# Causal mask of the first group by TensorE, and a reordered end of the last layers, in a float32 decoder

## Chip, cores, metric

One core of one Trainium2 chip. The time is the device time of one execution of the whole decoder in microseconds; lower is better. Everything is float32.

## What is computed

A decoder of two blocks on x (8 x 256 x 256): attention, cross attention and a mixture of experts, then the second block, with which the change is concerned. Each of its layers is followed by the sum with its input and a layer norm:

```
# second block: gated attention (16 heads of 16), MLP inside it, cross attention, channel mix
scores = einsum('bqhd,bkhd->bhqk', q, k) / sqrt(16)
scores = where(tril, scores, -inf);  attn = softmax(scores);  out = attn @ v
...
x_prev = concat([0, x[:, :-1]], axis=1)
xr = mu_r * x + (1 - mu_r) * x_prev
xk = mu_k * x + (1 - mu_k) * x_prev
out = sigmoid(xr @ W_r.T) * (square(relu(xk @ W_k.T)) @ W_v.T)
x = layernorm(x + out)
```

## The kernel before

The second block is one function, `last_layers`. The 2048 rows are 4 groups (G = 4) of 2 batch items, so a group has 4 tiles of 128 rows (NT = 4, HALF = 2). The groups go through a software pipeline of three stages: in period p group p is in attention (a), group p-1 in output product and MLP (r), group p-2 in cross attention and channel mix (z). Each engine has its own written program, a function per engine (`sync`, `gpsimd`, `tensor`, `scalar`, `vector`), strictly in order; semaphores join them (`wait_ge`, `then_inc`). The names of engines below are PE (TensorE), DVE (VectorE), ACT (ScalarE), POOL (GpSimd), SP.

*First group's attention (period 0).* Nothing else is in the pipeline yet, and the group is worked off in two halves, one batch item each. A half has 8 score units of 2 heads (`scores`, L1830 on). Unit j has the pair of banks 2(j mod 2) and the next one; its 4 products contract 32 rows each, so heads in different strips of 32 rows of the array can run side by side. Each bank gets 384 score columns (CAUSAL): 256 queries against the first 128 keys, 128 queries against the others. The two diagonal blocks of 128 x 128 are masked by DVE (`minimum`, L2889 on: the minimum with a tile of 3e38 and -1e30, in place in PSUM, 4 blocks a unit). Then ACT takes the exponential of the unit (`exponential`, L2442 on) and frees the banks (`s1e`). After every second unit but two steps late PE forms the weighted sum of values (`weighted`, L1846 on, bank 4), and ACT copies it (`heads_copy`). Before a half the PE turns the rotated queries and keys (`first_turns`, L1991) and DVE multiplies them with the gates' factors (`factors`, L2816 on). DVE's program of the first half holds the 8 minimums between its preparation of the second half (square sums, rotation, clock, norms); in the second half each minimum is followed by one `combine` (L2767) of the next group's rows, gathered from the experts' output by POOL. Then follow statistics, norm and turn of that front (`front_statistics`, `front_normalise`, ACT's `front_rows` L2398, PE's `turn_front`).

```
for j in range(PAIRS1 // GB, PAIRS1):      # DVE, second half of group 0
    minimum(0, j)
    combine(1, j - PAIRS1 // GB)
```

ACT's factors for the second half (`first_factors(1)`, L2515 to L2521) stand behind its eighth exponential. The flag `const` of POOL says that the masks and the ones in the values' tile are ready.

*The end.* After the periods the last group (LAST = 3) and the one before (OTHER = 2) are worked off with a program of their own. For the channel mix of the last group: PE turns the normed rows into a bank, ACT copies them shifted by one column (`mix_rows`, L2688), POOL subtracts shifted from unshifted (`last_difference`, L1758), DVE forms both mixes from the difference (`last_mix`, L3188), PE multiplies (`last_keys`, `last_receptance`), ACT takes relu and tanh (`last_activations`), DVE squares (`last_squares`, L3195), PE multiplies with W_v (`last_values`), and DVE forms the result (`last_result`, L3202 to L3207), statistics, and after POOL's root (`rstd`, L1667 and L1669) the norm (`last_norm`, L3181). Each step does one batch item, that is 2 tiles. The norm of OTHER stands in DVE's program between the results.

## Time and profile before

| | |
|---|---|
| median of 3 runs | 1203.19 us (1202.64 to 1204.02) |
| profiled execution, its own time | 1208.58 us |
| its span, first to last instruction | 1206.8 us |
| PE, DVE, ACT, POOL busy | 1103.5, 722.0, 548.7, 457.3 us |
| mean granted clock of PE | 0.967 |

### The profile page before, as it was taken

What the parts mean: (1) busy time and instruction counts of PE and PEld (TensorE: products, weight loads), DVE (VectorE), ACT (ScalarE), POOL (GpSimd) and SP (SyncE); (2) the same over time, 40 slices, a digit from 0 to 9 for tenths busy, and PEclk for the clock granted to TensorE, in tenths of its full rate; (3) what the DMA queues carried; (4) which work ended last, traced back from release to release, by engine and by line L of the source; (5) the groups of instructions that cost most, each with busy time, mean ns of one, the idle gap of its engine ahead of it and who ended that gap; (6) DMA issues with size and microseconds to landing.
All of it is one profiled execution on the core that took longest, in us unless ns stands there. A gap on an engine that the chain in (4) does not pass through costs nothing. (4 is left out here: it accounts for less than half of the span.)

```text
span 1206.8 us, 20429 instructions
## 1 busy us (share of the span) xinstructions
PE 1103.5 (91%) x6772; PEld 795.2 (66%) x6772; DVE 722.0 (60%) x2206; ACT 548.7 (45%) x1391; POOL 457.3 (38%) x535
## 2 busy tenths in 40 slices
PE   9899989998998997999999977789799899998996
PEld 4476457546744776999999964455565665565874
DVE  1482476348434845656565638658858787946456
ACT  1371265217322824333333337466576557643541
POOL 0160034006300974766666456025332432223022
PEclk9999999999999998999999989689999999999999
DMA  6000200020002033941111154000000100000001
GB/s 207 18 2 1 59 19 1 0 60 19 1 0 60 2 115 119 310 141 53 45 54 45 41 165 126 2 1 23 14 1 17 36 9 19 8 1 19 1 1 35
DMA packets 39997, 55.85 MB, mean 46 GB/s; under 512 B 6758, under 2 KB 32166, under 8 KB 39894
## 3 DMA queue, kind: packets, MB, share of 16 engines
q1 hardware_dynamic: 30598, 39.61, 10.1%
q0 software_dynamic: 3408, 9.31, 2.8%
q10 hardware_dynamic: 5888, 5.64, 1.5%
q8 instruction: 55, 0.90, 0.3%
q14 instruction: 48, 0.39, 0.1%
HBM read 43.76 MB, written 10.78 MB: 45 GB/s over the span
## 5 line engine op out<-in xcount | busy, mean ns | idle before, releaser
L1787 PE MATMUL bank<-words 128*128 128x256 f32 (+3 forms) x872 | 270.1, 461 | 20.4 <-ACT words L2391 3.7
L1787 PEld LDWEIGHTS bank<-words 128*128 128x128 f32 (+1 forms) x872 | 164.8, 196 | 99.2 <-issue 58.9
L464 PE MATMUL bank<-words 128*128 128x512 f32 x384 | 171.6, 595 | 0.1
L409 POOL TENSOR_TENSOR words<-words 128x256 f32<-128x256 f32 (+1 forms) x128 | 102.5, 829 | 151.8 <-DVE words L1090 151.2
L1297 PEld LDWEIGHTS bank<-words 128*128 128x128 f32 x1248 | 145.9, 193 | 3.5 <-ACT words L1333 1.6
L1297 PE MATMUL bank<-words 128*128 128x128 f32 x1248 | 146.4, 276 | 0.9 <-ACT words L1333 0.9
L787 ACT ACTIVATE words<-words 128x128 f32<-128x128 f32 (+1 forms) x256 | 112.8, 443 | 32.1 <-DVE words L923 32.0
L464 PEld LDWEIGHTS bank<-words 128*128 128x128 f32 x384 | 71.2, 191 | 78.6 <-issue 78.3
L779 ACT ACTIVATE words<-bank 128x512 f32<-128x512 f32 x48 | 28.7, 597 | 178.1 <-PE bank L464 178.1
L1348 ACT ACTIVATE words<-words 128x1024 f32 x39 | 41.1, 1057 | 137.1 <-PE bank L1297 98.4
L913 DVE COPY words<-bank 128x512 f32<-128x512 f32 x48 | 33.2, 691 | 92.2 <-PE bank L464 91.9
L923 DVE CUSTOM_DVE_ANT_0 words<-bank,words 128x128 f32<-128x128 f32 (+1 forms) x256 | 74.5, 349 | 7.2 <-PE bank L475 7.1
L1308 PE MATMUL bank<-words 128*128 x312 | 73.9, 380 | 0.7 <-DVE words L1397 0.7
L934 DVE COPY words<-bank 128x512 f32<-128x512 f32 x96 | 60.8, 685 | 15.8 <-PE bank L488 15.4
L475 PE MATMUL bank<-words 64*128 64x128 f32 (+1 forms) x512 | 54.2, 347 | 11.3 <-DVE words L923 7.9
L1254 POOL COPY words<-words 128x1024 f32 x39 | 40.3, 1035 | 60.3 <-PE bank L1297 60.3
L2447 ACT ACTIVATE words<-bank 128x768 f32<-128x768 f32 x64 | 48.9, 811 | 28.6 <-DVE bank L2892 28.4
L1308 PEld LDWEIGHTS bank<-words 128*128 128x128 f32 x312 | 56.2, 190 | 7.1 <-issue 1.1
L2892 DVE TENSOR_TENSOR bank<-bank,words 128x512 f32<-128x512 f32 x64 | 42.0, 693 | 27.9 <-PE bank L1842 25.9
L1393 DVE TENSOR_SCALAR words<-bank,words 128x128 f32<-128x128 f32 x156 | 44.0, 345 | 24.1 <-PE bank L1297 23.8
L130 POOL TENSOR_TENSOR words<-words 128x4 f32<-128x4 f32 x6 | 1.2, 202 | 148.2 <-DVE words L112 148.2
L488 PE MATMUL bank<-words 128*128 128x128 f32 x384 | 51.8, 282 | 6.1 <-POOL words L409 5.8
(357 smaller groups left out, 2003.5 us busy)
## 6 DMA issues: line engine op xcount, KB each, us to landing
words<-in_w SPq DMA_DIRECT2D x8, 1024.0 KB
y_slots<-words ACTq DMA_DIRECT2D x39, 128.0 KB
words<-in_w SPq DMA_DIRECT2D x8, 512.0 KB
words<-in_x SPq DMA_DIRECT2D x4, 512.0 KB, 4.1
x_rows<-words SPq DMA_DIRECT2D x16, 128.0 KB, 1.8
words<-in_wm SPq DMA_DIRECT2D x2, 1024.0 KB, 7.6
out_x<-words SPq DMA_DIRECT2D x16, 128.0 KB, 1.8
words<-in_xt SPq DMA_DIRECT2D x3, 512.0 KB, 3.8
```

Source lines behind the costliest of these rows:

```text
L409: last = pool.tensor_tensor(part, part, inv[:, j % SLOTS0, :, t:t + 1].to_broadcast([P, 2, P * (t + 1)]), ALU.mult)
L464: last = pe.matmul(bank[c % 2][:, :], w, r, start=k == 0, stop=k == KD - 1)
L475: last = pe.matmul(bank[SCORES[i % 2][n]][:, t * P:t * P + P * (t + 1)],  kt[r, m, b * S + t * P:b * S + (t + 1) * P], qt[r, m, b * S:b * ...
L488: last = pe.transpose(bank[2 + k][:, tok(i)], weights_of(j)[:, n, c:c + P], ident[:, :])
L787: last = act.activation(weights_of(i)[:, n, c], weights_of(i)[:, n, c], ACT.Exp, bias=negmax[:, i % SLOTS0, n, t:t + 1], scale=-1.0, accum ...
L923: last = dve.tensor_tensor_reduce(out=weights_of(i)[:, n, c], in0=bank[SCORES[i % 2][n]][:, c], in1=mask0[:, c], scale=-DH0 ** -0.5, scala ...
L934: dve.tensor_copy(turning[:, 512 * k:512 * k + 512], bank[2 + k][:, :]).then_inc(tcopied, 1)
L1297: last = pe.matmul(bank[(BANKG, BANKV)[half][j % 2]][:, c * P:(c + 1) * P], wfix[:, j % 2, k * 2 * FF + half * FF + c * P:k * 2 * FF + hal ...
L1308: last = pe.matmul(bank[BANKY[j % 2]][:, 0:D], hidden[:, j % 2, k * P:(k + 1) * P], w2[:, bass.ds(e * W2 + k * D, D)], start=k == 0, stop= ...
L1393: dve.tensor_scalar(value[:, c * P:(c + 1) * P], bank[BANKV[s]][:, c * P:(c + 1) * P], bias[:, bass.ds(e * 2 * FC + FC + c, 1)], 10.0, ALU ...
L1787: last = pe.matmul(out, w, r, start=i == 0, stop=i == len(pairs) - 1)
L2447: act.activation(es[:, j % 4, :, :], pair(j % 2)[:, :, 0:CAUSAL], ACT.Exp, scale=DH1 ** -0.5).then_inc(s1e, 1)
```

## The change

*Masks.* A new tile `below` (384 columns: 0 where a key may be seen, -1e30 where not, in both diagonal blocks) is filled by POOL with the other constants; it lies in the tile of the MLP, which is free until period 1. For group 0 `minimum` is gone. Instead PE starts each of a unit's two banks with a product of the identity and `below`, and the scores are summed onto it; the scores increment `s1m`, for which ACT waits. DVE's combines of group 1 now stand in a row. Groups 1 to 3 keep `minimum`.

*The end.* The mix of the last group is formed as mu x + (1 - mu) x_prev: ACT writes mu x from the turned bank (4 operations per batch item, behind its shifted copy), DVE adds (1 - mu) x_prev; POOL's difference is gone. ACT does both copies and activations batch by batch. DVE's order is a new one, with the statistics of OTHER moved up between the adds, and a mix between two adds. The norm of OTHER is applied by POOL. PE's receptance of batch 0 goes ahead of the turn of batch 1. The second batch item's values, result, statistics, root and norm go by tile.

```diff
@@ constants, POOL
+                pool.memset(below[:, :], 0.0)
...
+                for c in (slice(0, P), slice(S, CAUSAL)):
+                    pool.affine_select(out=below[:, c], in_=below[:, c], compare_op=ALU.is_ge,
+                                       fill=-1e30, base=0, pattern=[[1, P]], channel_multiplier=-1)
@@ end, POOL
-            def last_difference(b):
-                pool.wait_ge(n7.copied, 2 * LAST + b + 1)
-                pool.tensor_tensor(lastrl[:, :, batch(b)], x5t[:, :, b, 1:S + 1], x5t[:, :, b, 0:S], ALU.subtract).then_inc(lastapart, 1)
+            def older_norm(b):
+                rstd(OTHER, n8, b)
+                pool.drain()
+                for t in range(HALF * b, HALF * b + HALF):
+                    pool.tensor_scalar(x(OTHER, t), x(OTHER, t), n8.mv[:, t, 0:1], n8.inv[:, t:t + 1], ALU.subtract, ALU.mult).then_inc(n8.normed, 1)
...
+            rstd(LAST, n7, 0)
+            older_norm(0)
+            rstd(LAST, n7, 1)
+            older_norm(1)
+            rstd(0, n9, 0)
+            for t in rows_of_last:
+                last_rstd(t)
@@ PE
-                        last = pe.matmul(bank[n][:, part], ktm[r, odd, k0:k0 + P], qt[r, m, queries], start=True, stop=True)
-                last.then_inc(s1, len(units))
+                        last = pe.matmul(bank[n][:, part], ktm[r, odd, k0:k0 + P], qt[r, m, queries],
+                                         start=not masked, stop=keys == P or not masked)
+                last.then_inc(s1m if masked else s1, len(units))
...
+            def masked_scores(j):
+                if j >= 2:
+                    pe.wait_ge(s1e, j - 1)
+                for o in range(2):
+                    pe.matmul(bank[2 * (j % 2) + o][:, 0:CAUSAL], ident[:, :], below[:, :], start=True, stop=False)
+                scores(0, (j,), True)
...
-                        scores(0, (PAIRS1 // GB * b + j,))
+                        masked_scores(PAIRS1 // GB * b + j)
...
             last_keys(0, 6)
+            last_receptance(0, 7)
             last_turn(n7, 1, bank[5])
-            last_receptance(0, 7)
             last_values(0, 4)
             last_keys(1, 0)
             last_receptance(1, 2)
-            last_values(1, 5)
+            pe.wait_ge(lastkact, 2)
+            for t in rows_of_last:
+                product(bank[LASTVALUE[t]][:, 0:D], [(lastrl[:, k, tok(t)], wv2[:, k, :]) for k in range(KD)]).then_inc(lastv, 1)
@@ ACT
+            def scaled_rows_of(b, source):
+                for mu, dst in ((MUK, lastxk), (MUR, lastxr)):
+                    for k in range(KD):
+                        last = act.activation(dst[:, k, batch(b)].rearrange("p (t n) -> p t n", t=HALF), turned_rows(bank[source])[:, k, :, :],
+                                              ACT.Copy, scale=cols[:, mu, k:k + 1])
+                    last.then_inc(lastscaled, 1)
@@ DVE, first group
-            minimum(0, 0)
-            minimum(0, 1)
             square_sums(0, 2)
...
             for j in range(PAIRS1 // GB, PAIRS1):
-                minimum(0, j)
                 combine(1, j - PAIRS1 // GB)
@@ DVE, end
+            def last_mix(b, mu, dst):
+                dve.wait_ge(lastscaled, 2 * b + (1 if mu == MUK else 2))
+                for k in range(KD):
+                    last = dve.scalar_tensor_tensor(dst[:, k, batch(b)], x5t[:, k, b, 0:S], rest[:, mu - MUR, k:k + 1],
+                                                    dst[:, k, batch(b)], ALU.mult, ALU.add)
+                last.then_inc(lastmixed, 1)
...
+            statistics(OTHER, n8, rows_of_tiles(0))
             normalise(LAST, n7, lambda t: x(LAST, t), 0)
             add_product(LAST, n7, 2, bank[0])
+            last_mix(0, MUK, lastxk)
             add_product(LAST, n7, 3, bank[2])
-            last_mix(0)
+            last_mix(0, MUR, lastxr)
             normalise(LAST, n7, lambda t: x(LAST, t), 1)
+            last_squares(0, 6)
             older_result(1)
+            statistics(OTHER, n8, rows_of_tiles(1))
+            last_mix(1, MUK, lastxk)
+            last_mix(1, MUR, lastxr)
+            first_result(4)
             last_squares(1, 0)
+            last_statistics(rows_of_tiles(0))
+            for t in rows_of_last:
+                last_result(t)
+            for t in range(NT):
+                dve.wait_ge(n9.rstd, max(t, 1))
+                dve.tensor_scalar(x(LAST, t), x(LAST, t), n9.mv[:, t, 0:1], n9.inv[:, t:t + 1], ALU.subtract, ALU.mult).then_inc(n9.normed, 1)
```

Where the instructions stand. First PE's program at the start of the second half of the first group's attention, before; L1991 is the turn, L1842 the scores, L1853 the weighted sum, `x2` a repetition:

```order
L1991 MATMUL bank<-words 128x128 x8
L1842 MATMUL bank<-words 128x256 x2
L1842 MATMUL bank<-words 128x128 x2
L1842 MATMUL bank<-words 128x256 x2
L1842 MATMUL bank<-words 128x128 x2
L1842 MATMUL bank<-words 128x256 x2
L1842 MATMUL bank<-words 128x128 x2
L1842 MATMUL bank<-words 128x256 x2
L1842 MATMUL bank<-words 128x128 x2
L1853 MATMUL bank<-words 32x256 x4
L1853 MATMUL bank<-words 32x128 x4
```

and in the changed kernel, whose L2010, L1860 and L1872 are the same operations and L2018 the masks:

```order
L2010 MATMUL bank<-words 128x128 x8
L2018 MATMUL bank<-words 128x384 x2
L1860 MATMUL bank<-words 128x256 x2
L1860 MATMUL bank<-words 128x128 x2
L2018 MATMUL bank<-words 128x384 x2
L1860 MATMUL bank<-words 128x256 x2
L1860 MATMUL bank<-words 128x128 x2
L2018 MATMUL bank<-words 128x384 x2
L1860 MATMUL bank<-words 128x256 x2
L1860 MATMUL bank<-words 128x128 x2
L2018 MATMUL bank<-words 128x384 x2
L1860 MATMUL bank<-words 128x256 x2
```

Two mask products of 384 columns now stand ahead of the scores of each unit, and no two units stand side by side any more.

DVE in the second half, before: L2825 factors, L2892 minimum, L2767 combine:

```order
L2825 SCALAR_TENSOR_TENSOR words<-bank,words 128x2x128 x2
L2892 TENSOR_TENSOR bank<-bank,words 128x4x128
L2767 SCALAR_TENSOR_TENSOR words<-words 128x256
L2892 TENSOR_TENSOR bank<-bank,words 128x4x128
L2767 SCALAR_TENSOR_TENSOR words<-words 128x256
L2892 TENSOR_TENSOR bank<-bank,words 128x4x128
L2767 SCALAR_TENSOR_TENSOR words<-words 128x256
```

and now, L2861 factors, L2803 combine, L2942 and L2950 the statistics of the front:

```order
L2861 SCALAR_TENSOR_TENSOR words<-bank,words 128x2x128 x2
L2803 SCALAR_TENSOR_TENSOR words<-words 128x256 x8
L2942 BN_STATS words<-words 128x6 x2
L2950 BN_AGGR words<-words 128x2 x2
L2952 TENSOR_SCALAR words<-words 128x2
```

The combines stand in a row with nothing from PE to wait for.

The end of DVE's program, from the last adds of the cross attention (L2787, L2789) on, before; L3188 is the mix, L3234 and L3236 the result of OTHER, L3195 the squares, L3202 and L3204 the result, L3207 its statistics:

```order
L2797 BN_AGGR words<-words 128x2 x2
L3188 SCALAR_TENSOR_TENSOR words<-words 128x256 x4
L2781 TENSOR_SCALAR words<-words 128x256 x2
L3234 SCALAR_TENSOR_TENSOR words<-words,bank 128x512
L3236 SCALAR_TENSOR_TENSOR words<-words 128x512
L3188 SCALAR_TENSOR_TENSOR words<-words 128x256 x4
L3195 TENSOR_TENSOR words<-bank,words 128x2x256
L2774 BN_STATS words<-words 128x6 x2
L2797 BN_AGGR words<-words 128x2 x2
L2774 BN_STATS words<-words 128x6 x2
```

and the same part now; L3208 is the mix, L2817 the norm, L3215 the squares, L3268 and L3270 the result of OTHER, L2810 the statistics of OTHER:

```order
L3208 SCALAR_TENSOR_TENSOR words<-words 128x256 x2
L2823 TENSOR_TENSOR words<-bank,words 128x256
L2825 BN_STATS words<-words 128x6
L2833 BN_AGGR words<-words 128x2 x2
L3208 SCALAR_TENSOR_TENSOR words<-words 128x256 x2
L2817 TENSOR_SCALAR words<-words 128x256 x2
L3215 TENSOR_TENSOR words<-bank,words 128x2x256
L3268 SCALAR_TENSOR_TENSOR words<-words,bank 128x512
L3270 SCALAR_TENSOR_TENSOR words<-words 128x512
L2810 BN_STATS words<-words 128x6 x2
L2833 BN_AGGR words<-words 128x2 x2
L3208 SCALAR_TENSOR_TENSOR words<-words 128x256 x4
```

The keys' mix of batch 0 stands between two adds, and its squares ahead of the result of OTHER.

## Rows read from the trace of the kernel before

**Rows 1.** Page, costliest groups: line engine op count | busy us, mean ns, idle us.

```profile
L1787 PE MATMUL bank<-words 128*128 128x256 f32 (+3 forms) x872 | 270.1, 461 | 20.4 <-ACT words L2391 3.7
L1787 PEld LDWEIGHTS bank<-words 128*128 128x128 f32 (+1 forms) x872 | 164.8, 196 | 99.2 <-issue 58.9
```

**Rows 2.** Timeline, first score units: start us, length us, engine, line, form [idle before].

```profile
748.37 0.95 PE L1842 MATMUL bank<-words 32*128 32x256 f32 x16 [2.12 <-issue]
749.34 1.30 DVE L2892 TENSOR_TENSOR bank<-bank,words 128x512 f32<-128x512 f32 x2 [1.02 <-PE bank L1842]
```

**Rows 3.** Stretches: us, busy of PE, PEld, DVE, ACT, POOL; granted clock, DMA.

```profile
750.90:757.80 6.90, 6.86 (x64) 4.69 (x64) 5.12 (x10) 3.21 (x5) 1.27 (x1) 0.51 0.01 2
761.20:781.70 20.50, 14.48 (x126) 9.41 (x124) 13.36 (x26) 8.20 (x15) 0.00 (x0) 0.50 0.00 1
785.10:795.30 10.20, 6.18 (x34) 4.23 (x35) 6.12 (x25) 4.68 (x11) 2.25 (x3) 0.50 0.00 0
847.30:870.20 22.90, 19.32 (x242) 13.15 (x242) 19.06 (x44) 10.90 (x18) 8.87 (x11) 1.00 0.02 7
```

**Rows 4.** Chain of waits near the end: start us, us, what (256-column passes).

```profile
1134.53 10.56 PE bank L1787 x48
```

**Rows 5.** Timeline of PE, second period: 8 passes of 512 columns at full clock.

```profile
878.09 3.60 PE L1787 MATMUL bank<-words 128*128 128x512 f32 x8
```

**Rows 6.** Timeline of PE: two units and a sum (847 us), one unit (760 us).

```profile
847.31 0.93 PE L1842 MATMUL bank<-words 32*128 32x256 f32 x16 [0.83 <-issue]
848.17 0.86 PE L1853 MATMUL bank<-words 128*32 128x256 f32 x16
...
760.40 0.94 PE L1842 MATMUL bank<-words 32*128 32x256 f32 x8 [1.53 <-ACT words L2447]
761.27 1.51 PE L1853 MATMUL bank<-words 128*32 128x256 f32 x16
```

**Rows 7.** Timeline, between the halves of the first group's attention.

```profile
763.05 1.51 ACT L2447 ACTIVATE words<-bank 128x768 f32<-128x768 f32 x2 [2.43 <-DVE bank L2892]
...
767.06 1.94 PE L1991 MATMUL bank<-words 128*128 128x128 f32 x8 [0.57 <-DVE words L3007]
770.64 1.68 PE L1842 MATMUL bank<-words 32*128 32x256 f32 x16 [1.63 <-DVE words L2825]
```

**Rows 8.** Timeline, from the last weighted sum to the front's turn.

```profile
785.90 1.51 PE L1853 MATMUL bank<-words 128*32 128x256 f32 x16 [1.76 <-ACT words L2440]
...
787.47 0.38 ACT L2440 ACTIVATE words<-bank 128x256 f32<-128x256 f32 x1 [1.71 <-PE bank L1853]
...
789.87 0.91 ACT L2398 ACTIVATE words<-words 128x256 f32<-128x256 f32 x2 [2.02 <-DVE words L2933]
...
791.75 1.12 PE L1796 MATMUL bank<-words 128*128 128x128 f32 x4 [0.20 <-ACT words L2398]
```

**Rows 9.** Timeline, the end of the kernel.

```profile
1184.98 1.64 DVE L3188 SCALAR_TENSOR_TENSOR words<-words 128x256 f32<-128x256 f32 x4
...
1185.97 1.97 PE L1787 MATMUL bank<-words 128*128 128x256 f32 x8 [2.22 <-DVE words L3188]
...
1189.09 1.04 POOL L1758 TENSOR_TENSOR words<-words 128x512 f32<-128x512 f32 x1 [2.71 <-ACT words L2688]
...
1192.49 7.40 PE L1787 MATMUL bank<-words 128*128 128x256 f32 x32 [2.39 <-DVE words L3195]
...
1203.82 0.74 DVE L3181 TENSOR_SCALAR words<-words 128x256 f32<-128x256 f32 x2 [0.60 <-POOL words L1669]
```

**Rows 10.** Timeline, ACT's scaled copies of 128x256 from PSUM.

```profile
715.68 1.02 ACT L2359 ACTIVATE words<-bank,words 128x256 f32<-128x256 f32 x2 [0.53 <-PE bank L1796]
```

**Rows 11.** Timeline, POOL's selects and ACT's first copy behind the flag.

```profile
720.29 0.29 POOL L1652 TENSOR_SCALAR_AFFINE_SELECT words<-words 128x128 f32<-128x128 f32 x1
...
728.79 0.39 ACT L2429 ACTIVATE words<-bank 128x256 f32<-128x256 f32 x1
```

**Rows 12.** POOL by shape before 700 us, columns as in rows 1.

```profile
L392 POOL TENSOR_SCALAR words<-words 128x128 f32<-128x128 f32 x24 | 19.1, 794 | 0.0
```

More of the change, by code:

```diff
@@ L1436, in last_layers @@
         ones, tiny = sb([P, S]), sb([P, 1])
+        rest = sb([P, 2, KD])
         mask1, maskx = sb([P, P]), sb([P, S2])
@@ L1494, in last_layers @@
         m1pair, m1gelu, lastxq, lastxqr, lastbias = (sem("l_" + n) for n in ("m1pair", "m1gelu", "lastxq", "lastxqr", "lastbias"))
-        lastapart, lastmixed, lastkmm, lastrelu, lastkact, lastrmm, lastrsig, lastv, lastvr = (sem("l_last" + n) for n in (
-            "apart", "mixed", "kmm", "relu", "kact", "rmm", "rsig", "v", "vr"))
+        lastscaled, lastmixed, lastkmm, lastrelu, lastkact, lastrmm, lastrsig, lastv, lastvr = (sem("l_last" + n) for n in (
+            "scaled", "mixed", "kmm", "relu", "kact", "rmm", "rsig", "v", "vr"))
         PAIRS1, QUADS1 = GB * H1 // 2, GB * H1 // 4
@@ L1504, in last_layers @@
         LASTUP, LASTDOWN = ((4, 5, 0, 2), (1, 3, 4, 5)), (0, 2, 1, 3)
+        LASTVALUE = (4, 4, 5, 6)
         NE1, NW, NR = 5, 10, 5
@@ L1530, in rows_of @@
             return slice(HALF * b, HALF * b + HALF)
+        rows_of_last = range(HALF, NT)
         def batch(b):
@@ L1774, in _ @@
             last_bias(1)
-            for b in range(2):
-                rstd(LAST, n7, b)
-                last_difference(b)
-            for b in range(2):
-                rstd(OTHER, n8, b)
-            for b in range(2):
-                rstd(0, n9, b)
+            rstd(LAST, n7, 0)
[5 more added lines that the diff above has]
+                last_rstd(t)
         @block.tensor
@@ L1828, in form, with scores @@
                 product(bank[4 + i % 2][:, :], [(w[:, k, tok(c % 2)], xnt[:, k, :]) for k in range(KD)]).then_inc(fmm, 1)
-            def scores(g, units):
+            def scores(g, units, masked=False):
                 q = units[0] // 2
@@ L2751, in _ @@
             sums_copy(LAST, 3, (0, 2))
-            mix_rows(LAST, 0, 4)
-            mix_rows(LAST, 1, 5)
-            last_activations(0, 6, 7)
-            last_activations(1, 0, 2)
+            for b in range(2):
+                mix_rows(LAST, b, 4 + b)
+                scaled_rows_of(b, 4 + b)
+                last_activations(b, (6, 0)[b], (7, 2)[b])
         @block.vector
@@ L3175, in rows_of_tiles @@
                 return range(HALF * b, HALF * b + HALF)
-            def last_norm(b):
-                dve.wait_ge(n9.rstd, b + 1)
-                for t in rows_of_tiles(b):
-                    dve.tensor_scalar(x(LAST, t), x(LAST, t), n9.mv[:, t, 0:1], n9.inv[:, t:t + 1], ALU.subtract, ALU.mult).then_inc(n9.normed, 1)
-            def last_mix(b):
-                dve.wait_ge(lastapart, b + 1)
-                for mu, dst in ((MUK, lastxk), (MUR, lastxr)):
-                    for k in range(KD):
-                        last = dve.scalar_tensor_tensor(dst[:, k, batch(b)], lastrl[:, k, batch(b)], cols[:, mu, k:k + 1],
-                                                        x5t[:, k, b, 0:S], ALU.mult, ALU.add)
-                    last.then_inc(lastmixed, 1)
+            def last_mix(b, mu, dst):
[4 more added lines that the diff above has]
+                last.then_inc(lastmixed, 1)
             def last_squares(b, source):
@@ L3195, in last_squares, with first_result, last_statistics, last_result @@
                 dve.tensor_tensor(lastrl[:, :, batch(b)], both(source, b), lastrl[:, :, batch(b)], ALU.mult).then_inc(lastkact, 1)
-            def last_result(b, source):
-                h = slice(NT * LAST + HALF * b, NT * LAST + HALF * b + HALF)
-                dve.wait_ge(lastrsig, b + 1)
-                dve.wait_ge(lastv, b + 1)
-                dve.scalar_tensor_tensor(lastrs[:, rows_of(b), :], lastrs[:, rows_of(b), :], 1.0, both(source, b), ALU.add, ALU.mult)
+            def first_result(source):
+                h = slice(NT * LAST, NT * LAST + HALF)
+                dve.wait_ge(lastrsig, 1)
+                dve.wait_ge(lastv, 1)
+                dve.scalar_tensor_tensor(lastrs[:, 0:HALF, :], lastrs[:, 0:HALF, :], 1.0, both(source, 0), ALU.add, ALU.mult)
                 dve.drain()
-                dve.scalar_tensor_tensor(keep["x"][:, h, :], lastrs[:, rows_of(b), :], 0.5, keep["x"][:, h, :], ALU.mult, ALU.add)
+                dve.scalar_tensor_tensor(keep["x"][:, h, :], lastrs[:, 0:HALF, :], 0.5, keep["x"][:, h, :], ALU.mult, ALU.add)
                 dve.drain()
-                for t in rows_of_tiles(b):
+            def last_statistics(tiles):
+                for t in tiles:
                     dve.bn_stats(n9.bn[:, t, :], x(LAST, t))
-                averages(n9, rows_of_tiles(b))
+                averages(n9, tiles)
+            def last_result(t):
+                dve.wait_ge(lastrsig, 2)
+                dve.wait_ge(lastv, t)
+                dve.scalar_tensor_tensor(lastrs[:, t, :], lastrs[:, t, :], 1.0, bank[LASTVALUE[t]][:, 0:D], ALU.add, ALU.mult)
+                dve.drain()
+                dve.scalar_tensor_tensor(x(LAST, t), lastrs[:, t, :], 0.5, x(LAST, t), ALU.mult, ALU.add)
+                dve.drain()
+                last_statistics((t,))
+            dve.tensor_scalar(rest[:, :, :], cols[:, MUR:MUK + 1, :], -1.0, 1.0, ALU.mult, ALU.add)
             for t in range(NT):
```

25 lines of the change are left out of this document (7 added, 18 removed).

## Prediction

> **What bounds the kernel now.** The page first: the costliest group is PE's products, 872 passes with an idle time before them that is small, 20.4 us [rows 1], so work added to PE costs its own length unless PE waits at that place. Then the order of instructions in time, in the two places that the diff touches.
>
> *First group's attention (748 to 787 us).* A score unit is one pair of banks. Its cycle is PE, VectorE (DVE), ScalarE (ACT), PE: the scores are ready, DVE takes the minimum with the mask (two units in 1.30 us [rows 2]), ACT exponentiates (two in 1.51 us [rows 7]), and only then the pair of banks is free. PE waits here, and its granted clock stands at 0.50 to 0.51, the lower of its two levels (1.2 of 2.4 GHz), in most of both halves; in the later groups, whose attention is filled with the MLP's products, it is 1.00 [rows 3]. So this stretch is a ring of short dependent steps at half clock, not one of PE at its peak.
>
> *The end (1184 to 1207 us).* The shift by one token goes ACT, POOL, DVE, PE: after the last copy POOL subtracts for 1.04 us, then DVE mixes, PE had waited 2.39 us for the squares behind that mix, and after the last product, whose passes end at 1192.49 + 7.40 = 1199.89, DVE works to 1203.82 + 0.74 = 1204.56, a two-tile chain with POOL's root in it [rows 9].
>
> **Masks on PE, first half of the group.** Removed: 8 minimums of 0.65 us (1.30/2) from DVE [rows 2]. Added: 2 products of the identity with a 384-column mask per unit. A 256-column pass at full clock takes 10.56/48 = 0.22 us [rows 4] and a product is two passes; a 512-column pass 3.60/8 = 0.45 us with the last one's tail in it [rows 5]. 384 columns lie between: 0.22 x 1.5 = 0.33, 0.45 x 0.75 = 0.34, and as some of both is tail I take 0.325 us, so 4 passes or **1.3 us a unit**, 16 units 21 us of PE. At half clock it would be twice.
>
> The Trainium skill (TensorE: Matmul & The Clock Gate, section The mechanism) says that a weight load overlaps a running matmul only where the row groups differ; by that, each of the 64 passes would pay its load too. The trace disagrees: the 48 passes of [rows 4] use all rows, and 0.22 us each is no more than their columns take at 2.4 GHz.
>
> Scores: two units together take 848.17 - 847.31 = 0.86 us, but one unit alone also takes 761.27 - 760.40 = 0.87 us [rows 6], since its two row groups run side by side and the other two are idle. A full-array mask between the units ends that pairing. So a unit is 1.3 + 0.87 = 2.17 us. A weighted sum is 0.86 us long, about 0.8 us to the next start (my reading of the same rows; at half clock it is 1.51).
>
> The exponential of unit j and PE's work on unit j+1 overlap, and 2.17 us is longer than the 0.81 us of ACT, so PE never waits for a bank: it is the bound. The eighth unit's scores start 8 x 1.3 + 7 x 0.87 + 2 x 0.8 = 18.1 us after 748.37, its exponential starts 0.97 us later (the unit's 0.94 [rows 6] and a hand-over of 0.03, like the one of 748.37 + 0.95 to 749.34 [rows 2]), takes half of 1.51 and some, 0.81, and ends at 768.25; now that is 763.05 + 1.51 = 764.56 [rows 7]. **+3.7 us.** ACT's factors for the second half stand behind the eighth exponential, so what DVE is freed of (8 x 0.65 = 5.2 us) buys nothing here: DVE will wait for ACT.
>
> **Between the halves.** From that exponential to the next scores there are 770.64 - 764.56 = 6.1 us, with two turns of 1.94 us at half clock [rows 7]. PE comes to them warm, after two weighted sums: **-0.5 us** (none to -1).
>
> **Second half.** PE alone: 8 x 2.17 + 3 x 0.8 + 0.1 + 0.86 = 20.7 us. Now it is 785.90 + 1.51 - 770.64 = 16.8 us [rows 7, 8]. **+3.9 us.** But before it PE is nearly idle for some 4 us as DVE makes the factors, and after such idling the clock has been at its lower level here [rows 3]. I take 4 us at the lower level, which do 2 us of work: **+2.0 us** (0 to 3.4).
>
> **After the last weighted sum.** Now DVE's minimums and combines of the second group's rows alternate, statistics come last, and the turn of the front ends at 791.75 + 1.12 = 792.87, 5.4 us after the last sum's end [rows 8]. With the minimums gone, DVE has the whole second half for combines of the second group's rows, statistics and norm, all under PE's 20.7 us. What is late next is ACT, whose four row copies stand behind its last heads copy: 0.05 + 0.38 + 4 x 0.455 (two take 0.91, [rows 8]) + 0.5 = 2.8 us. **-2.6 us.** What follows PE did at 0.50 until 795.3 [rows 3]; warm, some of it shrinks: **-0.6 us** (0 to -1.2).
>
> **Constants.** POOL gets one fill and two more selects, 0.29 us each [rows 11], ahead of the flag; ACT's first copy that waits for it comes at 728.79, some 8 us after [rows 11]. Nothing, unless POOL is late by that much.
>
> **The end.** Each hand-over and DVE step here is read from the same part of the timeline as [rows 9]. Batch 0: ACT's two new copies with a scale take 1.02/2 = 0.5 us each from PSUM [rows 10], so after the shifted copy (which ends near 1182.7, 0.6 us after the turn) the keys' half is ready near 1183.7, and DVE mixes it in 0.82 us (half of 1.64) already between two adds, from 1183.9 on; PE's keys start near 1184.8, not 1185.97 [rows 9]. They end at 1186.6; the receptance, 1186.9 to 1188.7, the turn of batch 1 and the values of batch 0 follow without a stop. The norm of tiles 2 and 3 slips 0.7 us in return, as an add and the receptance mix now stand before POOL's root. POOL gets the older group's norms, 2 per batch; 128 columns of such an operation take it 0.79 us [rows 12], 256 of them perhaps 0.8 to 1.6; before its next root it has 4 us. Batch 1: PE is done with batch 0 by 1190.9; ACT copies from 1189.4 (after the turn and its tanh of 0.6 us), scales until 1190.95 and 1191.95; DVE, which in the meantime does the older result and its statistics, mixes until 1193.05; PE's keys and receptance, 16 passes of 0.23 (7.40/32), end at 1195.8 where they ended at 1199.89 less 8 such passes, about 1198.0. The values now come by tile, 4 passes or 0.9 us each: 1196.8 and 1197.7. DVE's work by tile is two products of 256 columns (0.42 each, by the first row of [rows 9]: 1.64/4), one bn_stats and one aggregation, and the hand-overs; I estimate 1.7 us: 1198.55 and 1200.25; then POOL's root, 1.2 us with its hand-overs as now, under which the first three tiles are normalised, and the last tile at 1201.5 to 1201.9. Now 1203.82 + 0.74 = 1204.56 [rows 9]. The stores behind are as before. **-2.7 us** (-4.2 to +0.5).
>
> **Sum.** +3.7 - 0.5 + 3.9 + 2.0 - 2.6 - 0.6 - 2.7 = **+3.2 us**. The profiled execution, 1208.58 us, would be 1211.8; it lies 5.4 us above the median, 1203.19, so the median would be **1206.4 us**. What a measurement of this kernel can tell from no change is 0.2%, 2.4 us: 1200.8 to 1205.6.
>
> **Rivals.**
> - *Faster, by packing.* If the score passes and the sums follow the masks without the hand-over that [rows 6] show, a unit's scores cost only their columns, (0.44 + 0.22) = 0.66 us, and the sums the same: -(15 x 0.21 + 5 x 0.14) = -3.9 us; PE is then dense enough that the pause between the halves leaves the clock up: -2.0. Together 3.2 - 5.9 = -2.7 us: 1200.5. For it: passes of one shape run without gaps [rows 4]. Against: one unit alone took 0.87 us at clock 1.00. It decides from 0.16 us a unit downward, given the clock. Chance 0.21. The Trainium skill (same page, section Why this matters for your kernels) asks for a PE that is not left idle between bursts if it is to keep its clock; by that the denser halves would gain, and no run so far tells whether the pause between them is short enough.
> - *No change.* The clock costs nothing (0 instead of +2.0) and the end gives 3.2: +0.7 us, 1203.9. Chance 0.26.
> - *More slower, at the end.* POOL's norms take 1.6 us and more beside DVE's work, the root of tiles 2 and 3 waits, and the gain at the end falls to 0.5: 1208.6. The Trainium skill (SBUF - State Buffer, section SBUF: two separate sides) says that POOL and DVE lock a shared pair of ports for a whole instruction, which would make this likelier; POOL's subtraction at 1189.09, beside idle DVE, took 1.04 us for 512 columns, so less than 0.8 us for 256 is likely, but no row has DVE busy beside it. Chance 0.10.
> - *Loads not hidden.* If a weight load of the page's 196 ns [rows 1] is paid on all 64 passes: +12.5 us, 1218.9. Chance 0.03.
> - *The masks themselves stay at half clock* (+21 us). 0.02: dense full-array passes have always come back to 1.00 in this trace.
>
> **How the numbers follow.** The forecast has 0.38; its own range, 1204.5 to 1209.5, comes from the unit's 2.1 to 2.25 us and the clock's 0 to 3.4. The range 1200.0 to 1211.0 takes in the first three rivals and the ends of the clock's term. Faster by over 0.2%: 0.21. Within: no change plus the low edge of the forecast, 0.30. Slower: 0.49.
>
> **What would show it.** In the changed kernel: mask products near 0.32 us a pass with the granted clock at 1.00; eighth exponential at 19 to 20 us after the first mask; DVE idle for ACT there; 18 to 23 us for the second half; 2.5 to 3.2 us from the last weighted sum to the end of the front's turn; the last DVE instruction 2 to 4 us nearer to the last context product. Wrong would be: PE waiting for ACT inside the halves, or mask passes at 0.65 us throughout.

## The result, and where the time went

The changed kernel takes **1213.62 us** (median of 4 runs, 1211.78 to 1214.80), the kernel before 1203.61 us beside it (4 runs, 1202.64 to 1205.56). The ratio is 1.0083, 95% interval 1.0069 to 1.0097: 10 us slower. The prediction had 1206.4 us in a range of 1200.0 to 1211.0. Its direction was right, its size and its range were not.

The profiled execution took 1214.54 us (span 1212.8). The stretches below are read from the timelines at the same events in both kernels. The second execution of the kernel before was profiled later, as `before_again`.

| stretch, us | before | before again | after | predicted change | measured change |
|---|---|---|---|---|---|
| half 1: first mask or scores to end of eighth exponential | 16.19 | 16.19 | 21.22 | +3.7 | +5.0 |
| to the next mask or scores | 6.08 | 6.07 | 5.73 | -0.5 | -0.35 |
| half 2: to the end of the last weighted sum | 16.77 | 16.76 | 28.81 | +5.9 | +12.0 |
| to DVE's first division behind the turn | 6.34 | 6.34 | 2.99 | -3.2 | -3.35 |
| all of periods 1 to 3 (not edited) | 383.8 | 377.5 | 380.2 | 0 | -3.6, +2.7 |
| end: first sum of the last cross attention to DVE's last end | 27.03 | 27.89 | 23.89 | -2.7 | -3.1, -4.0 |

The edited stretches add up to 5.0 - 0.35 + 12.0 - 3.35 - 3.1 = +10.2 us, close to the 10.0 us between the medians; the prediction's sum of the same terms was +3.2. How far this agreement is luck shows below, with `again`. Of the missing 7.0 us, 6.1 lie in half 2 and 1.3 in half 1.

PE in the changed kernel, from the timeline of PE (start us, length us, engine, line, form; in brackets the idle time before and what ended it):

```profile
747.56 1.56 PE L2018 MATMUL bank<-words 128*128 128x384 f32 x4 [2.20 <-DVE words L2861]
749.05 0.92 PE L1860 MATMUL bank<-words 32*128 32x256 f32 x8
749.90 1.56 PE L2018 MATMUL bank<-words 128*128 128x384 f32 x4
...
769.32 0.86 PE L1872 MATMUL bank<-words 128*32 128x256 f32 x16 [0.60 <-ACT words L2469]
771.40 1.17 PE L2010 MATMUL bank<-words 128*128 128x128 f32 x8 [1.22 <-DVE words L3043]
774.51 2.93 PE L2018 MATMUL bank<-words 128*128 128x384 f32 x4 [1.95 <-DVE words L2861]
777.37 1.65 PE L1860 MATMUL bank<-words 32*128 32x256 f32 x8
778.95 2.93 PE L2018 MATMUL bank<-words 128*128 128x384 f32 x4
...
802.46 0.86 PE L1872 MATMUL bank<-words 128*32 128x256 f32 x16 [0.60 <-ACT words L2469]
804.21 1.63 PE L1814 MATMUL bank<-words 128*128 128x128 f32 x8 [0.89 <-ACT words L2427]
```

The same stretch by windows (us; busy of PE, PEld, DVE, ACT, POOL with counts; granted clock; DMA share, GB/s): half 1 and the pause, the first part of half 2, the rest.

```profile
747.50:773.90 26.40, 23.19 (x168) 13.44 (x168) 13.13 (x23) 9.67 (x16) 3.81 (x3) 1.00 0.02 6
773.90:787.60 13.70, 13.09 (x36) 7.05 (x36) 8.78 (x30) 1.90 (x3) 2.27 (x3) 0.50 0.01 2
787.60:803.40 15.80, 15.12 (x128) 8.52 (x124) 0.00 (x0) 6.05 (x10) 0.00 (x0) 1.00 0.01 2
```

Three things stand here. The ring of [rows 2, 7] is gone: no row of a unit has an idle time before it, PE is the bound. In half 1 the clock is 1.00 where [rows 3] have 0.51 and 0.50, and still a unit takes 749.90 - 747.56 = 2.34 us, of which the masks are 749.05 - 747.56 = 1.49. And after the pause, in which PE has one row of turns between idle times of 1.22 and 1.95 us, the clock is at its lower level for 13.7 us, from 0.6 us ahead of the first mask on: a unit takes 778.95 - 774.51 = 4.44 us.

DVE has nothing left to do in half 1, and waits for ACT's factors (timeline, all engines):

```profile
767.97 0.81 ACT L2476 ACTIVATE words<-bank 128x768 f32<-128x768 f32 x1 [1.53 <-PE bank L1860]
...
769.96 0.69 DVE L3035 TENSOR_TENSOR words<-words 128x512 f32<-128x512 f32 x1 [12.54 <-ACT words L2546]
```

The end, in the places of [rows 9] (timeline, all engines):

```profile
1188.27 1.99 PE L1805 MATMUL bank<-words 128*128 128x256 f32 x8
...
1191.11 2.44 POOL L1776 TENSOR_SCALAR words<-words 128x256 f32<-128x256 f32 x2 [0.21 <-issue]
1191.56 1.56 ACT L2724 ACTIVATE words<-bank,words 128x256 f32<-128x256 f32 x4
...
1193.81 3.84 PE L1805 MATMUL bank<-words 128*128 128x256 f32 x16 [1.04 <-DVE words L3208]
...
1194.92 0.34 POOL L1676 TENSOR_TENSOR words<-words 128x2 f32<-128x2 f32 x1 [1.37 <-DVE words L2833]
...
1205.64 0.42 DVE L3237 SCALAR_TENSOR_TENSOR words<-words,bank 128x256 f32<-128x256 f32 x1 [0.36 <-PE bank L1805]
...
1207.24 0.42 DVE L3237 SCALAR_TENSOR_TENSOR words<-words,bank 128x256 f32<-128x256 f32 x1
...
1208.83 1.57 DVE L3316 TENSOR_SCALAR words<-words 128x256 f32<-128x256 f32 x4
```

The keys of batch item 0 (1193.81) and its receptance run in one row of 16 passes, where before the keys had a row of their own and a wait of 2.22 us. POOL's norm takes 2.44/2 = 1.22 us a tile and is done at 1193.55, 1.4 us before its next root. DVE's steps by tile are 1207.24 - 1205.64 = 1.60 us apart, and the last norm of four tiles is one row.

### The profile page after: what moved, and what is told of

Its sections match the earlier page's. It is cut to its first block and busy times, and to the rows that moved or that the text cites. A ratio compares the mean times of both kernels' runs of the same rounds, so it can differ in the third digit from the quotient of the medians.

```text
span 1212.8 us, 20562 instructions
## 1 busy us (share of the span) xinstructions
PE 1122.4 (93%) x6836; PEld 801.9 (66%) x6836; DVE 713.5 (59%) x2189; ACT 552.5 (46%) x1399; POOL 462.6 (38%) x542
## 3 DMA queue, kind: packets, MB, share of 16 engines
q1 hardware_dynamic: 30598, 39.61, 10.2%
## 5 line engine op out<-in xcount | busy, mean ns | idle before, releaser
L1676 POOL TENSOR_TENSOR words<-words 128x2 f32<-128x2 f32 x31 | 7.0, 226 | 144.1 <-DVE words L2833 144.0
```

## Which half of the change costs, and what the clock does

**The two parts by themselves.** `masks_only` has all edits but those of the end, `end_only` those of the end alone. Of the edit against the changed kernel two places stand here for each; the rest of it is the change's own diff taken back.

```diff
@@ masks_only: the end as before
-            last_receptance(0, 7)
             last_turn(n7, 1, bank[5])
+            last_receptance(0, 7)
...
@@ end_only: the masks as before
-                        masked_scores(PAIRS1 // GB * b + j)
+                        scores(0, (PAIRS1 // GB * b + j,))
...
+                minimum(0, j)
                 combine(1, j - PAIRS1 // GB)
```

> Only the masks move to TensorE; the end is that of before. Theory A (the masks cost 13 us, the end gives 3): 1216 to 1218 us, 12 to 14 us above before. Theory B (the end costs something too and the masks only some 10): 1211 to 1214 us.

> Only the end is new; the first group's masks stay with VectorE. Theory A: 3 us below before, 1200 to 1201.5 us, as the last VectorE instruction comes 3.1 us nearer to the last context products in the changed kernel's trace. Theory B: no gain or a loss, 1203 to 1205 us.

Beside 1207.54 us of the kernel before, `masks_only` took 1213.65 us (ratio 1.0051, 1.0031 to 1.0071) and `end_only` 1204.02 us (0.9973, 0.9957 to 0.9989). So the masks are the loss and the end a gain. As a difference, +6.1 us is less than either theory had for the masks, and -3.5 us is what theory A had for the end. The stretches give the sizes better than the ratios: with the old end the last stretch took 27.03, 27.89 and, in `masks_only`, 28.05 us, with the new one 23.9 in all 14 traces that have it. `masks_only` has the same 21.23 us in half 1 and 28.82 in half 2 as the changed kernel, `end_only` the 16.19 and 15.86 of the old ring. The ratios of the two parts, +0.51% and -0.27%, add up to less than the +0.83% of both together. The profiled execution of `masks_only` is no typical one: it is the slowest of seven, 1219.27 us at a mean granted clock of 0.976; only one other is like it (1218.35 us, 0.978), and the other five took 1209.87 to 1213.82 us at 0.982 to 0.985. These may have had a shorter stay at the lower clock, such as `again` shows below, but no trace shows them. Besides, the median of the kernel before itself lay between 1202.61 and 1208.37 us in the five comparisons, which is more than this gap: medians of different comparisons are not set against each other for a few us here.

**The same kernel again.** `again` and `third` are the changed kernel unedited, `before_again` the kernel before, for their traces.

> The changed kernel itself, timed beside the others of this call. 6 to 10 us above before.

> The changed kernel, a third trace: second half of the first group between 24 and 29 us as in the two others, the end 23.9 us from the first add of the cross attention to VectorE's last instruction.

> The kernel before once more, for a second trace: how much the stretch between the first group's attention and the end, which no part of the change touches, differs between two executions of one program. Theory: 2 to 4 us, all of it by the granted clock's dips; the first group's ring within 1 us of the first trace.

`again` took 1212.03 us (1.0078, 1.0064 to 1.0092); the single executions of `third` and `before_again` took 1216.00 and 1204.62 us. Half 1 is 21.23 us in all three traces of the changed kernel; half 2 is 28.81, 24.00 and 28.81. The windows of half 2 tell why (columns as above), of `again`:

```profile
775.00:778.85 3.85, 3.48 (x10) 1.74 (x12) 3.55 (x9) 0.00 (x0) 0.00 (x0) 0.57 0.01 4
778.85:799.60 20.75, 19.93 (x154) 11.37 (x150) 4.99 (x21) 8.09 (x13) 2.27 (x3) 1.00 0.01 2
```

and of `third`:

```profile
775.90:789.30 13.40, 12.77 (x34) 6.74 (x36) 8.80 (x30) 1.90 (x3) 2.26 (x3) 0.50 0.01 2
789.30:805.00 15.70, 15.10 (x126) 8.78 (x126) 0.00 (x0) 6.03 (x9) 0.00 (x0) 0.99 0.01 2
```

The clock falls in the pause every time. The windows that lie wholly at the lower level are, of `again` and of `third`,

```profile
774.90:778.30 3.40, 2.93 (x6) 1.25 (x6) 3.17 (x9) 0.00 (x0) 0.00 (x0) 0.50 0.02 5
775.93:789.57 13.64, 13.04 (x36) 7.01 (x36) 8.77 (x30) 1.90 (x3) 2.26 (x3) 0.50 0.01 2
```

so the way back took 3.4 us once and 13.6 us twice (in `masks_only` too), of the same instructions. One thing goes with it: the clock fell 0.60 to 0.62 us ahead of the first mask in the three traces with the long stay, and 0.48 to 0.49 us ahead of it in `again` and in the two spare runs below, which have the short one. No run moved this distance by itself, so it is not shown to be the cause.

With the short stay the edited stretches of `again` add up to 5.0 - 0.35 + 7.2 - 3.35 - 3.1 = +5.4 us, and yet this execution lies 9.2 us above the median before. Some 3.8 us of that come from stretches that no edit touches, which differ by as much between two executions of one program. So the equality of +10.2 and +10.0 above is in part luck. How many of the untraced executions of the changed kernel had the long stay is not known: of its nine timed in the two comparisons, five had a mean granted clock of 0.978 to 0.979 (1212.71 to 1214.80 us, the first profile among them) and four had 0.981 (1211.44 to 1212.03 us, `again` among them).

**Is it the pause?** `filler` puts products of no use (the identity with `below` into bank 5, which is free then) ahead of and behind the turns of the second half, 7 in all.

```diff
+            def filler(n):
+                for _ in range(n):
+                    pe.matmul(bank[5][:, 0:CAUSAL], ident[:, :], below[:, :], start=True, stop=True)
...
+                filler(3 * b)
                 pe.wait_ge(turning, HALF * b + HALF)
                 first_turns(b)
+                filler(4 * b)
                 pe.wait_ge(qkt, HALF * b + HALF)
```

> The changed kernel with 3 spare mask products (to an unused bank) before the turns of the second half and 4 behind them, so that TensorE is not idle while VectorE makes the factors. If the pause is what lets the clock fall, the granted clock stays at 1.00 in the second half, whose eight units then take 2.34 us each like the first half's: about 6.5 us less than the changed kernel, less at most 1 us that the filler delays the turns or scores: 1207 to 1209 us. If the clock falls for another reason (the masks themselves), it stays at 0.50 from 774 to 787 us and the time is 1213 to 1215 us.

Windows of `filler`: half 1, the pause, half 2.

```profile
750.00:772.00 22.00, 21.40 (x152) 12.32 (x156) 9.38 (x14) 8.35 (x14) 3.35 (x3) 1.00 0.02 7
772.00:777.00 5.00, 5.00 (x35) 3.26 (x28) 3.65 (x8) 1.21 (x3) 0.00 (x0) 1.00 0.01 3
777.00:801.00 24.00, 22.92 (x164) 13.06 (x162) 8.80 (x30) 8.35 (x14) 2.26 (x3) 1.00 0.01 1
```

PE is busy in all 5.00 us of the pause, and the clock stays at 1.00. Half 2 takes 22.51 us, the pause 6.82 instead of 5.73. This splits the 28.81: 22.5 is what the half takes with the masks at full clock, 6.3 the clock. Against the changed kernel the stretches give -6.3 + 1.1 = -5.2 us for the long stay at the lower level and -1.5 + 1.1 = -0.4 for the short one. By time it is 1208.89 us, ratio 1.0013 (0.9998 to 1.0028). The changed kernel was not timed beside it; `masks_only` was, at 1213.65 us, and less the 3.5 us of the end that is 1210.1 by estimate, 1.2 us above `filler`. So that the pause lets the clock fall is shown; what filling it is worth in the median lies between the two values. The Trainium skill (TensorE: Matmul & The Clock Gate, section Why this matters for your kernels) says that bursts of products must not be separated by idle gaps if the clock is to stay up. This pair of runs agrees, though that section speaks of longer single gaps than the two here, 1.22 and 1.95 us with a row of turns of 1.17 us between them.

**Is it what the products multiply?** Perhaps products of an identity and of zeros count for less than others. In `spare_dense` and `spare_mask` half 2 has two products of the same shape into bank 5 in place of the masks, of the MLP's weights or of identity and mask; DVE masks that half again. Both also wait for the weights ahead of the turns.

```diff
                 for o in range(2):
-                    pe.matmul(bank[2 * (j % 2) + o][:, 0:CAUSAL], ident[:, :], below[:, :], start=True, stop=False)
+                    if first_part:
+                        pe.matmul(bank[2 * (j % 2) + o][:, 0:CAUSAL], ident[:, :], below[:, :], start=True, stop=False)
+                    else:
+                        pe.matmul(bank[5][:, 0:CAUSAL], wm1[:, 0, 0:P], wm1[:, 0, P:P + CAUSAL], start=True, stop=True)
...
             for j in range(PAIRS1 // GB, PAIRS1):
+                minimum(0, j)
                 combine(1, j - PAIRS1 // GB)
```

> Second half of the first group: VectorE takes the minimum again (with its combines between), while TensorE computes in each unit, in place of the two mask products, two products of the same shape with dense weights and dense data, to an unused bank (one more wait for the weights). If the long time at the lower clock comes from mask products being almost all zeros, the clock is back at 1.00 within some 6 us of the first of them; if it comes from their shape, float32 and order, it stays at 0.50 for 10 to 13 us as in the changed kernel.

> The same with the identity and the mask as operands of the spare products. By both theories 10 to 13 us at 0.50 in the second half; time 1 to 3 us above the changed kernel. Against spare_dense it tells what the data does.

They took 1213.57 us (1.0088, 1.0073 to 1.0103) and 1211.09 us (1.0063, 1.0046 to 1.0081). The window after the pause, of `spare_dense`:

```profile
775.00:778.80 3.80, 3.41 (x8) 1.68 (x10) 0.33 (x1) 0.00 (x0) 0.00 (x0) 0.56 0.02 4
```

and of `spare_mask`:

```profile
774.70:777.50 2.80, 2.51 (x4) 1.18 (x4) 0.24 (x1) 0.00 (x0) 0.00 (x0) 0.50 0.03 6
```

Both were back after some 3 us, both had 24.6 us in half 2, and neither showed the 10 to 13 us at the lower level that was expected. The contents make no difference that these traces show. But both have the short stay, which the changed kernel has too in `again`, timed beside them; whether contents matter where the stay is long is not shown. Both also had 7.35 us behind the last weighted sum, where the changed kernel has 2.99: with the minimums back among the combines, DVE is late again. That is the term of -3.2 of the prediction, undone by itself.

## What a mask product costs

**Two units behind four masks.** `paired` makes the masks of two units in one go and then their scores.

```diff
-                for o in range(2):
-                    pe.matmul(bank[2 * (j % 2) + o][:, 0:CAUSAL], ident[:, :], below[:, :], start=True, stop=False)
-                scores(0, (j,), True)
+                for n in range(4):
+                    pe.matmul(bank[n][:, 0:CAUSAL], ident[:, :], below[:, :], start=True, stop=False)
+                scores(0, (j, j + 1), True)
```

> Masks of two units together, then the scores of both together. If each change between full-array masks and 32-row scores costs a hand-over of some 0.2 us and one unit's scores cost as much as two, a pair of units takes 8 x 0.32 + 0.2 + 0.86 = 3.6 us at full clock in place of 4.68: 4 us less per half, 1204 to 1207 us in all, if the clock behaves as in the changed kernel. If the hand-over isn't what the mask's 0.37 us per pass holds, and scores don't pair, no gain: 1212 to 1215 us.

Timeline of PE of `paired`, the first pairs:

```profile
746.58 2.85 PE L2018 MATMUL bank<-words 128*128 128x384 f32 x8 [2.12 <-DVE words L2861]
749.36 0.94 PE L1860 MATMUL bank<-words 32*128 32x256 f32 x16
751.92 2.85 PE L2018 MATMUL bank<-words 128*128 128x384 f32 x8 [1.63 <-ACT words L2476]
```

Eight passes take 2.78 us to the next start, four took 1.49. The difference, 1.29/4 = 0.3225 us, is the pass, as predicted (0.325). What is left, 1.49 - 4 x 0.3225 = **0.20 us**, comes once each time scores follow masks, and the prediction did not have it. The scores of two units run side by side again, in 0.87 us. Yet a cycle of two units is 751.92 - 746.58 = 5.34 us against 2 x 2.34 = 4.68 plus a weighted sum of 0.79 where there is one: now all four banks must be free before the masks start, so PE waits for ACT. Time 1209.25 us, ratio 1.0011 (0.9997 to 1.0024); neither expectation holds. Half 1 is as long as with the changed kernel (21.3 us), half 2 takes 25.63 us. The lower clock lasted 10.2 us, of which 6.2 lie in half 2 and the rest in the pause.

**Masks in bfloat16.** `bf16` multiplies bfloat16 copies of the identity and of the mask; the scores stay in float32.

```diff
+                pool.tensor_copy(below16[:, :], below[:, :])
+                pool.tensor_copy(ident16[:, :], ident[:, :])
...
-                    pe.matmul(bank[2 * (j % 2) + o][:, 0:CAUSAL], ident[:, :], below[:, :], start=True, stop=False)
+                    pe.matmul(bank[2 * (j % 2) + o][:, 0:CAUSAL], ident16[:, :], below16[:, :], start=True, stop=False)
```

> The changed kernel with the identity and the mask in bfloat16 (both exact there, -1e30 rounded), so a mask product is one pass of 384 columns. If it costs a quarter of the float32 one, 0.16 us, a unit takes 2 x 0.16 + 0.2 + 0.86 = 1.4 us at full clock, and a half of the group 14 us where before it took 16.2 to 16.8: 12 to 15 us below the changed kernel, 3 to 6 us below before. If a product has a floor or the clock stays low in both halves (PE less busy), no more than 5 us below the changed kernel.

Timeline of PE of `bf16`, a unit of half 1 and one of half 2:

```profile
748.88 0.50 PE L2024 MATMUL bank<-words 128*128 128x384 bf16 x2
749.31 0.92 PE L1866 MATMUL bank<-words 32*128 32x256 f32 x8
750.17 0.50 PE L2024 MATMUL bank<-words 128*128 128x384 bf16 x2
...
769.83 0.82 PE L2024 MATMUL bank<-words 128*128 128x384 bf16 x2
770.58 1.65 PE L1866 MATMUL bank<-words 32*128 32x256 f32 x8
```

and its window of half 2:

```profile
767.60:794.30 26.70, 25.21 (x149) 14.41 (x149) 6.91 (x26) 11.83 (x21) 2.26 (x3) 0.50 0.01 2
```

A product is one pass of half the length: two masks take 0.43 us instead of 1.49, a unit 1.29 instead of 2.34. Half 1 takes **12.77 us**, less than the 16.19 of DVE's ring. But half 2 takes 24.22 us: it begins at 766.10, the clock fell 1.1 us later, behind a pause of 5.73 us, and stayed down for all of this window, though PE was busy in 25.2 of its 26.7 us. The kernel is level with the one before, 1203.32 us, ratio 1.0008 (0.9991 to 1.0025).

**Both remedies.** `bf16_filler` adds 1 + 3 products in float32 around the turns to `bf16`; `bf16_paired_filler` makes the masks by pairs too; `both_fillers` has 3 more ahead of half 1; `bpf_again` repeats `bf16_paired_filler`. `end_filler` has the end's edits and DVE's old masks, with such products in the pause and behind each weighted sum.

```diff
@@ bf16_filler, bf16_paired_filler (both_fillers: filler(3, ...) in the first line)
+                filler(b, below[:, :])
                 pe.wait_ge(turning, HALF * b + HALF)
                 first_turns(b)
+                filler(3 * b, below[:, :])
@@ end_filler
                         weighted(0, QUADS1 // GB * b + (j - 3) // 2)
+                        filler(1, wqk[:, 0, 0:CAUSAL])
```

> The bfloat16 masks with spare float32 full-array products in the pause between the halves (1 before the turns, 3 behind them). In the run with the bfloat16 masks alone the clock fell in that pause and stayed at 0.50 for all of the second half, 24.2 us against 14.2 at full clock. If the pause is the cause: clock 1.00 all through, second half 14.2 us, 9 to 10 us below the bfloat16 masks alone: 1192 to 1195 us. If the 32-row scores themselves let it fall, it falls within the second half: 1198 to 1203 us.

> The same with two units' masks and then two units' scores together. A pair is then 4 x 0.16 + 0.2 + 0.86 = 1.7 us of TensorE, but waits for both exponentials, about 3.4 us a pair with the weighted sum against 2 x 1.28 + 0.8 = 3.36: the same time within 1.5 us as bf16_filler if the clock holds; with more pauses it may fall, then up to 8 us more.

> The masks stay with VectorE, the end is new, and spare float32 full-array products fill TensorE: 1 and 3 in the pause between the halves, one behind each weighted sum in both halves. If the lower clock is what costs the ring of before its time, the scores and sums run in half the time: 2 to 4 us below end_only, 1198 to 1202 us. If VectorE and ScalarE set the ring (the first half's minimums stand behind other work), no gain beyond 1 us.

> bf16_paired_filler with 3 spare float32 full-array products also in the pause ahead of the first half, where in the trace of bf16_filler the clock fell to 0.50 from 751 to 771 us (first half 20.4 us) and in others it did not. If that fall is what spreads the times, the clock is 1.00 in both halves in the trace and the median is 1 to 3 us below bf16_paired_filler with a narrower spread; if not, the same.

> The kernel bf16_paired_filler once more, beside both_fillers on the same chip: 10 to 13 us below before.

| kernel | us | before beside it | ratio (95%) | half 1, half 2 |
|---|---|---|---|---|
| `bf16_filler` | 1192.99 | 1202.61 | 0.9921 (0.9896 to 0.9946) | 20.37, 14.16 |
| `bf16_paired_filler` | 1191.18 | 1202.61 | 0.9901 (0.9883 to 0.9919) | 13.24, 14.53 |
| `bpf_again` | 1190.93 | 1208.37 | 0.9864 (0.9836 to 0.9892) | as above |
| `both_fillers` | 1190.91 | 1208.37 | 0.9863 (0.9834 to 0.9892) | 13.24, 14.52 |
| `end_filler` | 1205.72 | 1202.61 | 1.0024 (1.0013 to 1.0036) | 17.76, 15.53 |

Windows of `bf16_paired_filler`, as for `filler`:

```profile
748.00:762.00 14.00, 9.36 (x133) 5.56 (x137) 9.51 (x15) 7.69 (x14) 3.84 (x3) 1.00 0.04 11
762.00:767.00 5.00, 4.62 (x33) 2.50 (x26) 4.31 (x10) 1.27 (x3) 0.00 (x0) 1.00 0.00 0
767.00:782.00 15.00, 9.95 (x144) 5.82 (x144) 8.12 (x28) 7.62 (x14) 2.26 (x3) 1.00 0.01 2
```

Four products in the pause are enough here: half 2 falls from 24.22 us (`bf16`) to 14.16 and 14.53. `bf16_paired_filler` is **1191 us, faster than both kernels**, by 1.0 and 1.4% in its two comparisons. Against the kernel before its stretches are -2.95 (half 1), -0.46, -2.24 (half 2), -3.33, -3.13 (end): 12.1 us, where the medians differ by 11.4 and 17.4. In its two traces and in the one of `both_fillers` the clock is 1.00 in both halves and the pause. In the one trace of `bf16_filler` it fell 2.5 us into half 1, ahead of which PE had been idle for 2.12 us:

```profile
751.00:771.00 20.00, 19.40 (x124) 10.25 (x124) 7.31 (x11) 7.86 (x13) 1.75 (x2) 0.50 0.00 1
```

and was 1.00 again behind the filled pause. The same half 1 stayed at 1.00 in `bf16`, so the pairing is not shown to be what keeps it up. The six executions of `bf16_filler` range from 1188.88 us (mean granted clock 0.986) to 1198.86 (0.979), the profiled one at 1196.58 (0.978), so its median mixes executions with and without such a fall. The three products ahead of half 1 bring nothing by time. `end_filler`, 3.1 us above the kernel before, met neither of its expectations. With the masks on DVE half 2 gains 0.3 us on `end_only`'s 15.86, and half 1, the pause and the stretch behind the last weighted sum lose 1.6, 1.1 and 0.7 us. Here the products did not keep the clock up: it was at 0.50 in four pieces between 750 and 798 us, for 20.5 us in all, so what the ring of DVE and ACT would take at full clock was not seen.

## Why the prediction was wrong, by its own steps

- **"I take 4 us at the lower level ... +2.0 us (0 to 3.4)"** is the step that failed. The lower level held for 13.6 us in the changed kernel's profile, in `third` and in `masks_only`, and for 3.4 us in `again`; its price, measured against `filler`, is 6.3 us and 1.5 us. The fall itself was foreseen, from the right cause. The upper bound was not: it assumed that dense full-array work brings the clock back soon, and [rows 3] have no case of such work begun at the lower level with 32-row scores between. In the profiled execution this is 4.3 of the missing 7.0 us. Where the stay is short the term held, 1.5 us; yet `again` is 9.2 us slower too, and what its other 3.8 us are, in stretches without an edit, stays open.
- **The mask, "1.3 us a unit".** 1.49. The pass was right (0.3225 us against 0.325), the hand-over of 0.20 us to the scores was left out. This was so in every trace. Over 8 units it is the +1.3 us missing in half 1 (21.2 against 19.9, less 0.02 a unit where the scores were a little shorter than taken) and most of the 1.8 us in half 2 (22.5 against 20.7).
- **PE the bound in the halves, scores 0.87 us, DVE idle for ACT:** as predicted (0.85 us; DVE's idle time of 12.54 us).
- **Between the halves, -0.5:** -0.35. **After the last weighted sum, -2.6 and -0.6:** -3.35; `spare_mask` and `spare_dense` lose it again with the minimums among the combines, so it is the freed DVE; the clock's share, the -0.6, was not measured by itself. The turn ends 1.63 + 0.89 us behind the last sum, 2.5 us.
- **Constants, nothing:** the first masks start about where the first scores did (748.37 and 749.84 us before, 747.56 to 749.57 in the three traces of the changed kernel). No run tested it by itself.
- **The end, -2.7 (-4.2 to +0.5):** -3.1 to -4.0. ACT's scaled copies took 1.56/4 = 0.39 us, not 0.5; POOL's norm 1.22, inside 0.8 to 1.6 (the rival had held less than 0.8 to be likely); DVE's steps by tile 1.60, not 1.7.
- **The anchor.** The profiled execution before was 5.4 us above the median, and `before_again` shows where most of it may lie: 377.5 us in the unedited periods against 383.8. The sum stood on this execution and was shifted by 5.4 us. That +10.2 in the stretches met +10.0 in the medians looks like proof of the shift and is partly luck, as `again` shows with +5.4 and +9.2.
- **The rivals.** Packing: ruled out, the scores kept their 0.85 us and the sums 0.79. Loads not hidden: ruled out, passes of 256, 384 and 512 columns take 0.22, 0.3225 and 0.45 us, in step with their columns, with no room for a load of 0.196. The end as loser: ruled out. Masks wholly at half clock: ruled out as a whole, since 3 of the 16 units ran so. But between its +21 us and the +3.4 at which the clock's term ended no case was priced, and the 6.3 us of the profiled execution lie there; the range ended at 1211.0 because of that.

## What to carry over

A product that joins a chain of small ones is to be priced by three rows: its pass, the hand-over to the shape that follows, and the same at the lower clock. Where PE is idle for a few us and then becomes the bound, the length of the stretch at half clock is not readable from one trace; price it as lasting through the whole stretch as well as at the best case, or fill the pause. A mask of constants needs no float32: as bfloat16 products it cost less than a third (0.43 for 1.49 us), and it paid only once the pause was filled.

## What was not expected of the hardware

- A busy PE stayed at half clock. `bf16` had it busy for 25.21 of 26.70 us at 0.50, mostly with 32-row scores and 32-column sums; the changed kernel, whose units are mostly full-array float32 passes (2.86 of 4.44 us), came back after 3.4 or 13.6 us. What in this difference decides was not taken apart. Why one execution of the same program takes 3.4 and the next 13.6 us is open; the only difference seen is that of 0.1 us in how far ahead of the first mask the clock fell.
- The same program varies in places that no edit touched. The window 905 to 925 us of the kernel before has, in `before_again`,

```profile
905.00:925.00 20.00, 17.48 (x86) 10.36 (x85) 17.82 (x32) 12.83 (x36) 2.55 (x2) 1.00 0.08 26
```

  where the first profile had a granted clock of 0.91 there. Over 17 traces periods 1 to 3 took between 376.1 and 383.8 us.
- The hand-over between full-array and 32-row products costs 0.20 us in float32; in bfloat16 four masks take 0.75 us and two 0.43, so 0.11 is left. What it consists of was not tried.
